# Decay attention: scores computed a second time in a bank pair of their own, weighed a step later, exponential taken with the copy of the turned rows

## The reference, cut to what matters

```python
q, k, v = (proj(q_w, q_b), proj(k_w, k_b), proj(v_w, v_b))
scores = jnp.einsum('bhqd,bhkd->bhqk', q, k) / jnp.sqrt(jnp.float32(dk))
mask = jnp.tril(jnp.ones((s, s), bool))
p_ = jax.nn.softmax(jnp.where(mask, scores, -1e+32), axis=-1) * mask
distcum = jnp.cumsum(p_, axis=-1)
disttotal = p_.sum(-1, keepdims=True)
dist = jnp.sqrt(jnp.clip((disttotal - distcum) * pos, 0.0))
gamma = -jax.nn.softplus(gammas)[None]
total_effect = jnp.clip(jnp.exp(dist * gamma), 1e-05, 100000.0)
scores = jnp.where(mask, scores * total_effect, -1e+32)
p = jax.nn.softmax(scores, axis=-1)
out = jnp.einsum('bhqk,bhkd->bhqd', p, v)
```

## Time and profile before

| | |
|---|---|
| median of three runs | 2842.42 us (2832.82 to 2868.76) |
| the profiled execution's own time | 2857.05 us |
| its span | 2855.0 us |
| mean granted TensorE clock over the span | 0.77 |
| busy share of the span | PE 77%, DVE 58%, POOL 55%, ACT 48% |
| steps of the decay attention | 128, their first maxima from 1392.4 to 2632.2 us |

### The profile page before, as it was taken

How to read it: one execution, slowest core, us unless ns; L and a number is a source line. 1 busy time by engine, 2 the same in 40 slices (tenths; PEclk the granted TensorE clock), 3 DMA queues, 4 the chain that set the end, 5 groups by cost and what they waited for, 6 DMA issues and landing times. The chain is left out here.

```text
span 2855.0 us, 51907 instructions
## 1 busy us (share of the span) xinstructions
PE 2188.2 (77%) x18588; PEld 1560.4 (55%) x18588; DVE 1660.3 (58%) x3445; ACT 1367.6 (48%) x2802; POOL 1579.8 (55%) x1921
## 2 busy tenths in 40 slices
PE   6999499999400099993598888888888888888385
PEld 5888367777300055551365555656656555665274
DVE  4898367777560044444366667666666666667424
ACT  1443156666300044441356666666566666656332
POOL 6563034444137734441777777686676876655271
PEclk9998589999655599996667777676676776666587
DMA  1110220000001255551000000000000000000002
GB/s 45 39 40 20 94 85 2 2 2 2 2 21 52 78 141 148 145 148 49 11 4 5 4 4 5 4 5 4 5 4 5 4 5 4 1 1 1 4 1 60
DMA packets 97275, 89.85 MB, mean 31 GB/s; under 512 B 55373, under 2 KB 82893, under 8 KB 97040
## 3 DMA queue, kind: packets, MB, share of 16 engines
q0 software_dynamic: 21616, 49.41, 6.0%
q1 hardware_dynamic: 75424, 37.32, 5.0%
HBM read 55.90 MB, written 30.79 MB: 30 GB/s over the span
## 5 line engine op out<-in xcount | busy, mean ns | idle before, releaser
L1471 POOL TENSOR_TENSOR d_decay<-d_later,d_posg 128x768 f32<-128x768 f32 x128 | 232.3, 1815 | 321.3 <-DVE d_later L1870 321.3
L1512 PE MATMUL d_T<-ident,d_p 128*128 128x128 f32 x768 | 170.2, 344 | 171.6 <-ACT d_pT L1646 100.7
L1870 DVE TENSOR_TENSOR_SCAN d_later<-d_cont,d_ex 128x768 f32<-128x768 f32 x128 | 230.9, 1804 | 76.6 <-ACT d_ex L1664 76.6
L1512 PEld LDWEIGHTS d_T<-ident,d_p 128*128 128x128 f32 x768 | 112.5, 174 | 244.5 <-issue 232.8
L1831 DVE TENSOR_REDUCE d_mx<-d_S 128x4 f32<-128x512 f32 x128 | 88.5, 692 | 252.5 <-PE d_S L1499 252.5
L1282 DVE TENSOR_TENSOR e_cont<-e_h,e_upto 128x512 f32<-128x512 f32 x91 | 62.9, 691 | 282.6 <-ACT e_upto L1181 282.6
L1499 PEld LDWEIGHTS d_S<-d_kT,d_qT 16*128 16x128 f32 x2048 | 172.4, 249 | 65.0 <-issue 65.0
L1499 PE MATMUL d_S<-d_kT,d_qT 16*128 16x128 f32 (+1 forms) x2048 | 192.7, 343 | 0.0
L1105 PE MATMUL e_X<-ident,e_xt 128*128 128x128 f32 x182 | 40.1, 302 | 197.9 <-DMA e_xt<-sent_rows 197.9
L1659 ACT ACTIVATE d_decay<-d_decay 128x768 f32<-128x768 f32 x128 | 107.3, 838 | 154.0 <-POOL d_decay L1411 154.0
L1068 POOL DMA_INDIRECT sent_rows<-moe_rows,slot x128 | 125.1, 977 | 101.2 <-DVE slot L1258 62.5
(11 more groups left out here) (375 smaller groups left out, 6267.5 us busy)
## 6 DMA issues: line engine op xcount, KB each, us to landing
sent_rows<-b_blank SPq DMA_DIRECT2D x14, 845.0 KB, 11.1
e_xt<-sent_rows SPq DMA_DIRECT2D x91, 130.0 KB, 2.6
back_rows<-e_ys SPq DMA_DIRECT2D x91, 64.0 KB, 1.6
out_h<-g_Y SPq DMA_DIRECT2D x8, 512.0 KB, 4.0
rows<-in_table,idx POOLq DMA_INDIRECT x128
sent_rows<-moe_rows,slot POOLq DMA_INDIRECT x128, 2.3
d_moe<-back_rows,slot POOLq DMA_INDIRECT x128, 2.5
e_wt<-in_pair_w,e_pair POOLq DMA_INDIRECT x91
```

The costliest lines, as they stand in the source:

```text
L1471: pool.tensor_tensor(decay[u][:], later[u][:, 0:2 * SEG].rearrange("p (e s) -> p e s", e=2), posg[:, h:h + 2, :], ALU.mult).then_inc(U["pl ...
L1512: last = nc.tensor.transpose(bT[:, t * P:(t + 1) * P], p2[K % KEEP_P][:, e, t * P:(t + 1) * P], ident[:])
L1870: nc.vector.tensor_tensor_scan(later[u][:, 1:1 + 2 * SEG], cont[:], ex[u][:].rearrange("p e s -> p (e s)"), 0.0, ALU.mult, ALU.add)\
```

## The change

It lies in `phase_decay_attention` alone.

- The scores are computed twice. `scores(K, bank)` takes the bank pair as an argument: `d_S` for the maxima and the first softmax, `d_R` for the weighing. The two pairs of before are now one pair for each use.
- In iteration K, PE issues `scores(K + 1, bS)` and then `scores(K - 1, bR)`, both behind the second turn of step K-3. The first waits for `shifted` of step K, the second for `weighed` of step K-2.
- The weighing of step K-2 stands in DVE's iteration K, between the subtraction and the scan (before: that of step K-1, behind the scan). `d_decay`, `d_qT` and `d_kT` have three buffers instead of two.
- POOL's "placed" of step K-1 moves from the end of iteration K-1 to the start of iteration K, and the subtraction in `d_p` to the end of the iteration.
- ACT no longer exponentiates `d_p`; the copy of the turned rows (`keep_turned`) is an exponential instead. `d_ex` and the three functions for `d_decay` stand behind the second copy.
- The `WARM` matmuls and their constant are gone.

```diff
-    WARM = 4
+    KEEP_Q, KEEP_D = 3, 3
...
-        bS = [m_.ps(f"d_S{u}", [P, 2, 512]) for u in range(2)]
+        bS, bR = [m_.ps(f"d_{name}", [P, 2, 512]) for name in ("S", "R")]
...
                     if step_there(K - 1):
-                        u = (K - 1) % 2
+                        u, d, h = (K - 1) % 2, (K - 1) % KEEP_D, 2 * ((K - 1) % PAIRS)
+                        pool.wait_ge(U["scanned"], K)
...
+                        pool.tensor_tensor(decay[d][:], later[u][:, 0:2 * SEG].rearrange("p (e s) -> p e s", e=2),
+                                           posg[:, h:h + 2, :], ALU.mult).then_inc(U["placed"], 1)
...
-                def scores(K):
+                def scores(K, bank):
...
-                    if K >= 2:
-                        pe.wait_ge(U["weighed"], K - 1)
                     for e in range(2):
-                        nc.tensor.matmul(bS[u][:, e, 0:SEG], ident_b[:], hide[:], start=True, stop=False)
+                        nc.tensor.matmul(bank[:, e, 0:SEG], ident_b[:], hide[:], start=True, stop=False)
...
-                    if step_there(K):
-                        scores(K)
-                        if quad_there((K - 6) // 2):
-                            pe.wait_ge(Q["attT_kept"], (K - 6) // 2 + 1)
-                        for _ in range(WARM):
-                            nc.tensor.matmul(bO[:], ident_b[:], fill[:], start=True, stop=True)
...
+                    if step_there(K + 1):
...
+                        if K >= 0:
+                            pe.wait_ge(U["shifted"], 2 * (K + 1))
+                        scores(K + 1, bS).then_inc(U["scored"], 1)
+                    if step_there(K - 1):
+                        if K >= 2:
+                            pe.wait_ge(U["weighed"], K - 1)
+                        scores(K - 1, bR).then_inc(U["rescored"], 1)
...
-                    nc.scalar.activation(pT[w % KEEP_T][:], bT[:, 0:SEG], ACT.Copy).then_inc(U["pT_kept"], 1)
+                    nc.scalar.activation(pT[w % KEEP_T][:], bT[:, 0:SEG], ACT.Exp).then_inc(U["pT_kept"], 1)
...
-                    if step_there(K - 2):
-                        w = (K - 2) % KEEP_P
-                        act.wait_ge(U["shifted2"], K - 1)
-                        nc.scalar.activation(p2[w][:], p2[w][:], ACT.Exp).then_inc(U["exped2"], 1)
...
+                    if step_there(K - 2):
+                        u, w, d = K % 2, (K - 2) % KEEP_P, (K - 2) % KEEP_D
+                        dve.wait_ge(U["rescored"], K - 1)
+                        dve.wait_ge(U["decay_made"], K - 1)
...
+                        nc.vector.scalar_tensor_tensor(p2[w][:], decay[d][:], 1e-5, bR[:, :, 0:SEG],
+                                                       ALU.max, ALU.mult).then_inc(U["weighed"], 1)
```

More of the change, by code:

```diff
@@ L1331, in phase_decay_attention @@
         hT, hTr = m_.sb("d_hT", [P, 2 * P]), m_.sb("d_hTr", [P, SEG])
-        qT = [m_.sb(f"d_qT{u}", [P, 2, 4 * P]) for u in range(2)]
-        kT = [m_.sb(f"d_kT{u}", [P, 2, 2 * P]) for u in range(2)]
+        qT = [m_.sb(f"d_qT{u}", [P, 2, 4 * P]) for u in range(KEEP_Q)]
+        kT = [m_.sb(f"d_kT{u}", [P, 2, 2 * P]) for u in range(KEEP_Q)]
         v = [m_.sb(f"d_v{u}", [P, 6, NH, STRIP]) for u in range(KEEP_V)]
@@ L1336, in phase_decay_attention @@
         rtot = [m_.sb(f"d_rtot{u}", [P, 2, 2, 2]) for u in range(2)]
-        ex, decay = [[m_.sb(f"d_{name}{u}", [P, 2, SEG]) for u in range(2)] for name in ("ex", "decay")]
+        ex = [m_.sb(f"d_ex{u}", [P, 2, SEG]) for u in range(2)]
+        decay = [m_.sb(f"d_decay{u}", [P, 2, SEG]) for u in range(KEEP_D)]
         later = [m_.sb(f"d_later{u}", [P, 1 + 2 * SEG]) for u in range(2)]
@@ L1464, in _ @@
                             pool.tensor_tensor(xn[:], hc[:], over(rstd[:], D), ALU.mult).then_inc(G["xn_made"], 1)
-                    if step_there(K):
-                        u = K % 2
-                        h = 2 * j
-                        pool.wait_ge(U["scanned"], K + 1)
-                        if K >= 2:
-                            pool.wait_ge(U["weighed"], K - 1)
-                        pool.tensor_tensor(decay[u][:], later[u][:, 0:2 * SEG].rearrange("p (e s) -> p e s", e=2),
-                                           posg[:, h:h + 2, :], ALU.mult).then_inc(U["placed"], 1)
+                    if step_there(K - 2):
+                        u, w = (K - 2) % 2, (K - 2) % KEEP_P
+                        pool.wait_ge(U["max2_made"], 2 * (K - 1))
+                        pool.tensor_tensor(long(p2[w]), long(p2[w]), wide(mx2[u], 1, P), ALU.subtract)
+                        pool.tensor_tensor(short(p2[w]), short(p2[w]), wide(mx2[u], 0, HALF), ALU.subtract)\
+                            .then_inc(U["shifted2"], 1)
             @block.tensor
@@ L1830, in _ @@
                             dve.wait_ge(U["exped"], K - 1)
[L1831 to L1832 removed]
+                        nc.vector.tensor_reduce(mx[u][:, 1], long(bS), AX, ALU.max).then_inc(U["max_made"], 1)
+                        nc.vector.tensor_reduce(mx[u][:, 0], short(bS), AX, ALU.max).then_inc(U["max_made"], 1)
                         dve.wait_ge(U["max_made"], 2 * K + 1)
```

99 lines of the change are left out of this document (42 added, 57 removed).

## The result

The changed kernel takes 3066.4 us (median; 3038.93 to 3083.3), the kernel before 2855.59 us beside it: a ratio of 1.076, with a 95% interval of 1.062 to 1.089. Forecast were 2836 us and, at the outside, 2935 us. The profiled execution took 3038.93 us with a span of 3037.1 us.

A forecast was written before the change was run, and what follows sets the result against it. PE's work at its granted clock and a chain returning to PE were taken to bound the kernel. 11.4 - 1.96 + 0.25 = 9.69 us a step, about 6 us gained with the ends, gave 2836 us; range 2710 to 2935 us.

The forecast's parts named there:

- T = W - 0.85 b + w: Attention stage: step time from PE's low-clock work, fast busy time and idle time; forecast 11.4 - 1.96 + 0.25 = 9.69 us.
- W: PE's work per step in low-clock time: 10.4 us before, less 1.68 for constant products, plus 2.66 for second scores: 11.4.
- b: PE's busy time per step at the high clock: forecast 2.3 us, from about one and a half rises per four steps.
- w: PE's idle time per step: forecast 0.25 us, from a shortfall of 0 to 0.5 us at the high clock.
- A bank pair for each use, weighing a step later: PE no longer stands for the weighing; the chain through scores, scan and weighing is cut, leaving 0.25 us idle a step.
- Rival 3: Without constant products, two score blocks in a row lose PE's clock: T 10.48 us, 92 us more, 2934 us; chance 0.22.
- Rival 2: PE's clock gains in part as falls become fewer: b 3.6, T 8.64 us, 142 us less, 2700 us; chance 0.24.
- Rival 1: PE's clock stays high once it has no waits; POOL binds at 7.7 us: 262 us less, 2580 us; chance 0.08.
- Rival 4: The chain through PE's second turn binds, as ACT's d_ex exponential follows the second copy: 64 us more, 2906 us; chance 0.04.
- ACT: Dropping 128 exponentials of 0.834 us is worth nothing by itself; the exponential from PSUM takes 0.49 us, like the copy.
- POOL: Same five operations a step, reordered, busy 7.3 us; binds only if T falls to about 7.7, so costs nothing.
- The ends: The last step is weighed one iteration later, with an emptying pipeline: 3 us more, between 0 and 9.7.

The follow-up runs named there:

- `d_y` first: Changed kernel with DVE's normalising of the attention's result (d_y) moved ahead of the maxima: 2914.41 us, ratio 1.018 to the kernel before.
- second scores at the head: Changed kernel with the second scores at the start of PE's next iteration, between turning back and first turn: 2972.84 us, ratio 1.046 to the kernel before.
- both: Changed kernel with d_y ahead of DVE's maxima and the second scores at the start of PE's next iteration: 2796.68 us, ratio 0.982 to the kernel before.
- both, early exponential: Changed kernel with d_y ahead of the maxima, second scores heading PE's iteration, and ACT's d_ex exponential ahead of both copies: 2765.19 us, ratio 0.967.
- mask alone, `d_y` first: Changed kernel with d_y ahead of the maxima and the second scores' products left out from the third step, only the mask written: 2812.6 us, ratio 0.985.
- before, no constant products: Kernel before the change with WARM set to 0 and nothing else changed: 2899.77 us, ratio 1.014.
- before, scores doubled: Kernel before the change with mask and scores issued twice into the same bank pair in place of the constant products: 3130.77 us, ratio 1.100.
- its mirror: Kernel before the change with d_y moved from behind the subtraction to behind the scan, weighing and second maxima on DVE: 3140.41 us, ratio 1.104.

## Why the prediction was wrong

The form T = W - 0.85 b + w held, as far as this check can tell. T, w (the idle time) and the clock are read from the stretch between the first and last first maxima; W is 10.4 for before, 11.4 with second scores, 9.5 with the mask alone and 8.7 without the constant products; b follows from the form. The row of the kernel before fits by construction, since its W was worked out that way. In the others the time at the high level, (2 x clock - 1) x T, is read apart from the form and has to lie between b and b + w:

| kernel | T | w | clock | b by the form | high-level time | b + w |
|---|---|---|---|---|---|---|
| forecast | 9.69 | 0.25 | 0.63 | 2.3 | 2.55 | 2.55 |
| before | 9.76 | 1.43 | 0.70 | 2.44 | 3.90 | 3.87 |
| after | 11.21 | 2.05 | 0.65 | 2.64 | 3.36 | 4.69 |
| `d_y` first | 10.01 | 0.71 | 0.65 | 2.47 | 3.00 | 3.18 |
| second scores at the head | 10.58 | 2.20 | 0.73 | 3.55 | 4.87 | 5.75 |
| both | 9.24 | 0.95 | 0.74 | 3.66 | 4.43 | 4.61 |
| both, early exponential | 8.87 | 0.61 | 0.75 | 3.69 | 4.44 | 4.30 |
| mask alone, `d_y` first | 9.41 | 1.71 | 0.68 | 2.12 | 3.39 | 3.83 |
| before, no constant products | 10.10 | 2.58 | 0.63 | 1.41 | 2.63 | 3.99 |
| before, scores doubled | 11.57 | 2.33 | 0.65 | 2.54 | 3.47 | 4.87 |

It does in every row but that of the fastest kernel, which is 0.14 us over (two digits of the clock allow 0.09). Where w is large this is a weak check, since the bounds lie w apart. A stronger one lays PE's busy time over the changes of the granted clock in the trace. The changed kernel is then busy 2.93 us a step at the high level and 6.23 at the low one, which makes W = 6.23 + 1.85 x 2.93 = 11.6. All kernels with second scores come out at 11.5 to 11.7, and the kernel before at 10.7. So W stands, each value some 0.2 to 0.3 us higher than in the table, and so does the added work (0.9 us for 0.98).

One premise of the prediction does not stand: that nearly all of the idle time lies at the high level. Before the change 1.05 of 1.43 us did; in the changed kernel it is 0.49 of 2.05 us.

- **The step that failed is w**, in the part "A bank pair for each use, weighing a step later": 2.05 us a step in place of 0.25, which is 1.80 x 127 = 229 us too little. I worked out the chain from the subtraction to the next scores, which the change names, and not the wait for `d_y`, whose row (68.7 us) stood in the earlier trace rows. What it took to see this could be had from what was there. The order of instructions showed that both turns now come ahead of both score blocks, so nothing stands on PE between turning back and the next turn. DVE's program had the weighing and the second maxima moved in front of `d_y`. Two questions were not asked: what was the moved step covering, and what is now queued ahead of the instruction that releases it? The undo takes 152 us off, with the wait down to 50.4 us, and its mirror in the kernel before adds 287 us: that shows the cause.
- **W was right** within 0.3 us. But "each 0.1 us of PE work per step is 12.7 us" was wrong: 1.9 us less work gave 102 us, not 241, since PE's idle time grew in its place and b fell.
- **b and the clock were near**: 2.64 by the form (2.93 by the trace, with its W of 11.6, which gives the same T) for 2.3, and 0.65 for 0.63. This would have made the kernel 37 us faster than forecast; with w too small by 229 us the sum is off by 192, and the profiled execution is off by 188 us (3038.93 less 2851). The rest of the 230 us between the medians is that the median of these runs lies 27 us above the profiled one, where I had taken 15 us below.
- **Rival 3 (slower, the clock is lost)** came out on the right side for another reason: b is 2.64 and not 1.2. The constant products did hold the clock up (0.70 to 0.63 without them), but two score blocks a step need not pull it down: with the second one at the head of the iteration, apart from the first, the clock is 0.73 to 0.75 in three kernels, above that of the kernel before. With the two in a row it was 0.65 each time (changed kernel, `d_y` first, scores doubled), so that part of the rival is not refuted.
- **Rival 2's clock (0.73)** came true only in the reordered kernels, at T of 10.58, 9.24 and 8.87 for its 8.64.
- **Rival 1 and the page's rule.** With `d_y` first PE idles 0.71 instead of 2.05 us a step, and the clock stays at 0.65; with the second scores at the head it idles 2.20 us at a clock of 0.73. By the rule of the Trainium skill ("TensorE: Matmul & The Clock Gate", section "HAM oscillation"), that idle stretches bring the slow clock, the first should have been the faster-clocked of the two. The traces disagree: PE has 11 pauses of over 1 us in the stage with `d_y` first, and 62 with the second scores at the head. From 1609.9 to 1630.0 us of the kernel with `d_y` first PE is busy 20.1 of 20.1 us, and the clock is 0.50 throughout. So rival 1, that the clock stays high once PE has no waits, is refuted.
- **Rival 4** was put at 64 us and a chance of 0.04, and it was worth 31 us in the kernel with both edits. In the changed kernel more than half of DVE's wait ahead of the scan is the wait for `d_y` handed on, since the exponential stands behind a copy that stands behind the late turn: with `d_y` first it is 228.0 us, for 488.7.
- **ACT** was right twice: the exponential from PSUM costs what the copy costs, and 107 us less of ACT's work gained nothing (ratio 1.007).
- **POOL** at 7.3 us a step was right for the changed kernel (906.2 / 127 = 7.14), but "binds only if T falls to about 7.7" took its busy time as fixed. In the fastest kernel it is 8.08 of 8.87 us, and with POOL kept apart from the scan 6.81 (865.2 / 127): part of its busy time is waiting beside the scan. Whether POOL or PE (8.26 us busy) binds the fastest kernel is not shown.
- **The ends** took 6.5 us more for the 3 forecast, inside 0 to 9.7.

## What to carry to other kernels

A moved piece of work leaves a hole: for each wait of the bounding engine that is listed before the change, even a short one, look up what stood between the wait's cause and the wait, and whether it still stands there. Then walk the releasing engine's program down to the instruction that releases, and count all that is now ahead of it; 0.6 us of work behind 3.9 us of other work cost 5% here (152 of 3066 us). Work put in as cover does not cover if it only leaves its old place ahead of the cause of the wait: the engine then comes to the wait sooner, and is released no sooner.

## What the runs showed of the hardware

**The granted clock does not follow from how busy TensorE is.** The same instructions in two orders gave 0.65 and 0.73 (changed kernel, and with the second scores at the head) at an idle time of 2.05 and 2.20 us a step. PE's order alone does not fix it either: with both edits it was 0.74 at 0.95 us of idle time, and with POOL's subtraction held back behind the scan, PE's program unchanged, 0.65 at 0.84 us. Which neighbourhood of pieces or pauses does it is open; no run varied one piece at a time.

**A scan on DVE and elementwise work on POOL hold each other up.** The timeline of the changed kernel:

```profile
2026.65 0.73 POOL L1451 TENSOR_TENSOR H<-H,d_cb 128x256 f32<-128x256 f32 x1
2026.69 3.31 DVE L1874 TENSOR_TENSOR_SCAN d_later<-d_cont,d_ex 128x768 f32<-128x768 f32 x1
...
2027.34 1.03 POOL L1468 TENSOR_TENSOR d_p<-d_p,d_mx 128x512 f32<-128x512 f32 x1
2028.34 2.06 POOL L1469 TENSOR_TENSOR d_p<-d_p,d_mx 128x256 f32<-128x256 f32 x1
```

The scan takes 1.76 us where POOL is idle beside it (all 89 such scans of this trace lie between 1.758 and 1.762 us; the other 39 take 2.93 in the mean) and 3.31 here: it ends at 2030.00, which is 1.63 us behind the end of POOL's second piece at 2028.37. POOL's third piece takes 2.06 us in place of the 0.61 it takes alone and ends at 2030.40, 0.40 us behind the end of the scan. Both distances are a little shorter than the times alone (1.76 and 0.61), so the three ran one after another, or nearly, though their rows overlap. The Trainium skill says so ("SBUF — State Buffer", section "SBUF: two separate sides"): an operation of VectorE with two SBUF inputs and one of GpSimd that reads SBUF take the shared ports in turn, each for its whole length. The trace agrees. It shows besides that here the waiting scan did not get in between two POOL instructions in a row: its row begins at 2026.69, ahead of the second POOL piece.
